# A transformer block on one core: attention output normalised with channels on partitions, its numerators and inverse sums moved by DMA, in place of transposes

## What is computed

```python
h = x @ W1 + b1                                   # q, k, v
w = softmax(q @ k.T / sqrt(8), causal)
a = (w @ v) with the heads side by side           # (512, 128)
x = layernorm(x + a @ Wp + bp)
r = sigmoid(xr @ W_r.T);  k = xk @ W_k.T          # xr, xk: x mixed with the token before it
x = layernorm(x + r * (relu(k)**2 @ W_v.T))
```

## Time and profile before

| what | us |
|---|---|
| device time, median of 3 runs (lowest, highest) | 766.25 (763.33, 769.27) |
| the profiled execution: device time | 766.06 |
| the profiled execution: span, first to last instruction | 764.3 |
| PE busy, share of the span | 621.4, 81% |
| DVE busy | 557.7, 73% |
| ACT busy | 471.6, 62% |
| POOL busy | 378.4, 50% |
| mean granted TensorE clock | 0.959 of full |

### The profile page before, as it was taken

One profiled execution on the slowest core, in us unless ns is written; L12 is line 12 of the kernel. 1 busy time (PEld: TensorE's weight loads), 2 busy tenths in 40 slices (PEclk: granted clock), 3 DMA queues, 4 the chain that ended last, 5 costly groups with the idle time before them and its releaser, 6 DMA issues.

```text
span 764.3 us, 18024 instructions
## 1 busy us (share of the span) xinstructions
PE 621.4 (81%) x6733; PEld 279.5 (37%) x6733; DVE 557.7 (73%) x1644; ACT 471.6 (62%) x918; POOL 378.4 (50%) x520
## 2 busy tenths in 40 slices
PE   2256987998988989898989898988989898977743
PEld 2013233434343435343434434343435343433232
DVE  3067777778888887879797978788887978782231
ACT  1111676586767676677777686767676766677510
POOL 6110334355655655565556464655655565455533
PEclk9999999999999999999999999999999999999755
DMA  1241213132331323241413141332323231100100
GB/s 47 96 97 49 94 54 104 44 92 66 79 93 58 112 58 115 45 124 34 118 38 118 40 127 45 75 96 58 112 59 113 54 104 29 47 17 16 29 14 14
DMA packets 65500, 53.19 MB, mean 70 GB/s; under 512 B 10882, under 2 KB 61316, under 8 KB 65412
## 3 DMA queue, kind: packets, MB, share of 16 engines
q1 hardware_dynamic: 65412, 52.03, 24.5%
HBM read 34.70 MB, written 17.30 MB: 68 GB/s over the span
## 4 chain that ended last, share of the span: by engine, by line
PE 60%; DVE 21%; ACT 8%; issue 5%; POOL 2%; DMA 2%; SPq 1%; POOLq 0%; DVEq 0%; ACTq 0%
PE ops L510 15%; DVE rowmax L661 12%; PE sps L487 10%; PE tps L451 10%; PE spare L390 8%; ACT probs L592 6%; PE spare L404 5%; PE sps L472 3%; DVE h L714 3%; PE spare L430 2%; PE spare L417 2%; PE spare L420 1%; PE spare L402 1%; DVE y L703 1%; PE spare L427 1%
## 5 line engine op out<-in xcount | busy, mean ns | idle before, releaser
L661 DVE TENSOR_REDUCE rowmax<-sps 128x1 f32<-128x512 f32 (+7 forms) x1024 | 401.3, 448 | 103.0 <-PE sps L487 102.2
L592 ACT ACTIVATE probs<-tps 128x512 f32<-128x512 f32 x640 | 346.4, 595 | 149.9 <-PE tps L451 149.9
L761 POOL TENSOR_SCALAR_AFFINE_SELECT probs<-probs 128x512 f32<-128x512 f32 x256 | 158.0, 635 | 272.6 <-ACT probs L592 272.6
L510 PE MATMUL ops<-probs,vop 128*32 128x384 f32 (+3 forms) x2048 | 175.7, 450 | 5.5 <-POOL probs L761 4.2
L451 PE MATMUL tps<-qop,kop 50*128 50x384 bf16 (+3 forms) x1024 | 127.5, 307 | 39.9 <-ACT probs L592 36.1
L487 PE MATMUL sps<-kop,qop 48*64 48x512 bf16 (+7 forms) x2048 | 130.6, 310 | 11.9 <-DMA kop<-d_parts 11.9
L472 PE MATMUL sps<-qmask,dup 64*128 64x128 bf16 (+1 forms) x640 | 69.7, 215 | 38.2 <-DVE rowmax L661 34.0
L451 PEld LDWEIGHTS tps<-qop,kop 50*128 50x128 bf16 x1024 | 34.3, 94 | 164.2 <-ACT probs L592 111.5
L510 PEld LDWEIGHTS ops<-probs,vop 128*32 128x32 f32 x2048 | 50.5, 109 | 79.9 <-issue 61.2
L487 PEld LDWEIGHTS sps<-kop,qop 48*64 48x64 bf16 x2048 | 43.1, 106 | 54.5 <-issue 19.6
L472 PEld LDWEIGHTS sps<-qmask,dup 64*128 64x128 bf16 x640 | 31.4, 95 | 80.6 <-DVE rowmax L661 74.2
(11 more groups left out here) (70 smaller groups left out, 601.7 us busy)
## 6 DMA issues: line engine op xcount, KB each, us to landing
d_parts<-qk_parts SPq DMA_DIRECT2D x16, 768.0 KB, 3.8
qop<-d_parts SPq DMA_DIRECT2D x192, 32.0 KB
qop<-d_parts SPq DMA_DIRECT2D x64, 96.0 KB
kop<-d_parts SPq DMA_DIRECT2D x192, 32.0 KB
kop<-d_parts SPq DMA_DIRECT2D x64, 96.0 KB
xa<-L_attn_x SPq DMA_DIRECT2D x16, 256.0 KB, 3.0
xres<-L_attn_x SPq DMA_DIRECT2D x16, 256.0 KB, 3.4
out<-result SPq DMA_DIRECT2D x16, 256.0 KB, 2.5
```

Of the source, the lines that this page charges most:

```text
L510: last = nc.tensor.matmul(ops[32 * t:32 * t + 32, BLK * a:SEQ], vop[:, par, a, QUARTET * half + t, hh, :], probs[:, g % 2, i, off:off + w] ...
L592: nc.scalar.activation(probs[:, g % 2, i, :], tps[:, bank(4 * GROUPS * n + 4 * g + i), :], ACT.Exp, scale=SCALE)\
L661: last = nc.vector.reduce_max(rowmax[:, par, QUARTET * half + i, a:a + 1], sps[:, bank(n), off:off + w], axis=AX_X)
L761: last = nc.gpsimd.affine_select(out=v, in_=v, compare_op=ALU.is_ge, fill=0.0, base=0, pattern=[[0, QUARTET], [1, BLK]], channel_multiplie ...
```

## The change

The numerators and sums stay with channels on partitions, as they leave PSUM, and DMA does the regrouping:

- In vop the columns of ones stand right behind each head's eight columns of v, so that ops holds for each head eight rows of numerators and eight rows of its sum. This is only an order of columns.
- The uses sums0, sums1 and attnT of spare are gone, with their transposes, DVE's reciprocals and products (L692, L695) and ACT's copy (L566).
- `move_o` (SP): osum of a half is stored to DRAM (256 KB), and after it has landed the 64 rows of numerators are read to numer (128 KB) and one row of sums per head to sums, spread over 128 partitions (16 KB, pieces of 128 bytes). Half 1 stands between the operand loads of half 1 and load_max of half 1; half 0 between the operand loads of half 0 and load_max of half 0.
- `invert_sums` (DVE, group 3): one reciprocal, 128x64, for both halves.
- `spread_inverses` (SP, behind the issue of xres and ahead of d_parts): the inverses go to DRAM (32 KB), and after that has landed they are read back with each head's row repeated on eight partitions (256 KB).
- `divide_attn` (POOL, group 4, behind the mask of group 4): one product numer by inv_rows, 128x512, straight into attnT. PE waits for it before project.

Of the diff, the declarations of the new semaphores are left out.

```diff
@@ -47,6 +47,7 @@
 PARTS = 3
+SHARE = PAIRS * SEQ // P
 LOADED = 16 * 2 * 2 * 4
@@ -63,13 +64,12 @@
     (1, 0): ("T", "max1"), (1, 1): ("A", "k"),
-    (2, 0): ("E", "key"), (2, 1): ("D", "sums1"),
-    (3, 0): ("E", "gate"), (3, 1): ("D", "attnT"),
+    (2, 0): ("E", "key"),
+    (3, 0): ("E", "gate"),
     (4, 1): ("E", "value"),
     (8, 0): ("D", "hT"),
-    (8, 1): ("T", "sums0"),
 }
@@ -183,8 +183,10 @@
         osum = sb("osum", [P, 2, SEQ])
-        inv = sb("inv", [P, 2, TT, QUARTET, 2])
-        attn = sb("attn", [P, TT, HEADS, DH])
+        sums = sb("sums", [P, 2, SHARE])
+        inv = sb("inv", [P, 2, SHARE])
+        inv_rows = sb("inv_rows", [E, SEQ])
+        numer = sb("numer", [E, SEQ])
         attnT = sb("attnT", [E, SEQ])
@@ -214,6 +216,9 @@
         d_max = nc.dram_tensor("d_max", (2, MROWS, 2, MAXIMA, QBLK), BF16, kind="Internal").ap()
+
+        d_o = nc.dram_tensor("d_o", (2, PAIRS, 2, DH, SEQ), F32, kind="Internal").ap()
+        d_inv = nc.dram_tensor("d_inv", (2, PAIRS, SEQ), F32, kind="Internal").ap()
 
@@ -318,6 +329,31 @@
 
+            def move_o(n, half):
+
+                wait(sp, o_copied, 2 * n + half + 1)
+                wait(sp, numer_in[half], 16 * n)
+                wait(sp, sums_in[half], 16 * n)
+                sp.dma_start(d_o[half].rearrange("h s d n -> (h s d) n"), osum[:, half, :])\
+                    .then_inc(o_out[half], 16)
+                wait(sp, o_out[half], 16 * (n + 1))
+                wait(sp, attn_done, n)
+                sp.dma_start(numer[E // 2 * half:E // 2 * half + E // 2, :],
+                             d_o[half, :, 0]).then_inc(numer_in[half], 16)
+                wait(sp, inv_done, n)
+                sp.dma_start(sums[:, half, :], d_o[half, :, 1, 0].rearrange("h (c n) -> h c n", n=SHARE))\
+                    .then_inc(sums_in[half], 16)
+
+            def spread_inverses(n):
+
+                wait(sp, inv_done, n + 1)
+                wait(sp, inv_in, 16 * n)
+                sp.dma_start(d_inv.rearrange("f h (c n) -> (h c) f n", n=SHARE), inv[:]).then_inc(inv_out, 16)
+                wait(sp, inv_out, 16 * (n + 1))
+                wait(sp, attn_done, n)
+                sp.dma_start(inv_rows[:], d_inv.rearrange("f h n -> (f h) n").unsqueeze(1)
+                             .to_broadcast([HEADS, DH, SEQ])).then_inc(inv_in, 16)
+
             def step(b, par):
@@ -326,6 +362,8 @@
                     load_operands(other, 1)
+                if active("D", b):
+                    move_o(before("D", b), 1)
                 if active("T", b):
@@ -334,6 +372,7 @@
                     sp.dma_start(xres[:], x[b + OFFSET["D"]].rearrange("(t p) e -> p t e", p=P)).then_inc(xres_in, 16)
+                    spread_inverses(before("D", b))
                 if active("A", b):
@@ -350,6 +389,8 @@
                     load_operands(par, 0)
+                if active("T", b):
+                    move_o(before("T", b), 0)
                 if active("S", b):
@@ -410,16 +451,8 @@
                     last = rowmax_transpose(par, 1)
-                elif use in ("sums0", "sums1"):
-                    half = int(use[-1])
-                    wait(pe, o_copied, 2 * before(stage, b) + half + 1)
-                    for t in range(TT):
-                        last = nc.tensor.transpose(spare[:, P * t:P * t + P], osum[:, half, P * t:P * t + P], ident)
-                elif use == "attnT":
-                    for t in range(TT):
-                        last = nc.tensor.transpose(spare[:, P * t:P * t + P],
-                                                   attn[:, t].rearrange("q h d -> q (h d)"), ident)
                 elif use == "project":
+                    wait(pe, attn_done, before("D", b) + 1)
                     last = tokens_by_weights(attnT, wp[:])
@@ -546,7 +579,7 @@
                 stage, use = SPARE_USES.get((g, place), (None, None))
-                if stage is None or not active(stage, b) or use in ("sums0", "sums1", "project", "value"):
+                if stage is None or not active(stage, b) or use in ("project", "value"):
                     return
@@ -560,10 +593,8 @@
                     for hh in range(2):
-                        ins = nc.scalar.copy(vop[:, 1 - par, :, :, hh, DH * hh:DH * hh + DH],
+                        ins = nc.scalar.copy(vop[:, 1 - par, :, :, hh, 2 * DH * hh:2 * DH * hh + DH],
                                              spare[:].rearrange("k (t p h d) -> k h t p d", t=TT, p=PAIRS, h=2)[:, hh])
-                elif use == "attnT":
-                    ins = nc.scalar.copy(attnT[:], spare[:])
                 elif use in ("q", "k"):
@@ -593,8 +624,8 @@
 
-            def copy_o(n, half, taken):
-                wait(act, spare_written, taken)
+            def copy_o(n, half):
+                wait(act, o_out[half], 16 * n)
                 wait(act, pv_done, GROUPS * n + CHUNKS * (half + 1))
@@ -617,9 +648,9 @@
                     if g == 1 and active("D", b):
-                        copy_o(before("D", b), 1, last_use(b, "sums1"))
+                        copy_o(before("D", b), 1)
                     if g == CHUNKS + 1 and active("T", b):
-                        copy_o(before("T", b), 0, last_use(b, "sums0"))
+                        copy_o(before("T", b), 0)
                     if active("T", b):
@@ -684,18 +715,6 @@
                                                    ALU.add, ALU.subtract).then_inc(spare_read, 1)
-                elif use in ("sums0", "sums1"):
-
-                    half = int(use[-1])
-                    wait(dve, spare_written, written)
-                    tiles = spare[:].rearrange("q (t r s h d) -> q s t r h d", t=TT, r=QUARTET, s=2, h=2)
-                    nc.vector.reciprocal(inv[:, half], tiles[:, 1, :, :, :, 0]).then_inc(inv_done, 1)
-                    wait(dve, inv_done, 2 * n + half + 1)
-                    for t in range(TT):
-                        last = nc.vector.tensor_tensor(
-                            attn[:, t, DH * half:DH * half + DH].rearrange("q (r h) d -> q r h d", h=2),
-                            tiles[:, 0, t], inv[:, half, t].unsqueeze(3).to_broadcast([P, QUARTET, 2, DH]), ALU.mult)
-                    last.then_inc(spare_read, 1)
                 elif use == "project":
@@ -708,6 +727,12 @@
 
+            def invert_sums(n):
+                for half in range(2):
+                    wait(dve, sums_in[half], 16 * (n + 1))
+                wait(dve, inv_out, 16 * n)
+                nc.vector.reciprocal(inv[:], sums[:]).then_inc(inv_done, 1)
+
             def normalise(i, n, src, dst, done_rstd, done):
@@ -721,6 +746,8 @@
                     spare_use(b, par, g, 0)
+                    if g == 3 and active("D", b):
+                        invert_sums(before("D", b))
                     if g == 7 and active("D", b):
@@ -748,7 +775,7 @@
                 last = nc.gpsimd.memset(vop[:].rearrange("k b t p h c -> k (b t p) h c")[
-                    :, :, hh, (2 + hh) * DH:(3 + hh) * DH], 1.0)
+                    :, :, hh, (2 * hh + 1) * DH:(2 * hh + 2) * DH], 1.0)
             last.then_inc(vop_cleared, 1)
@@ -786,6 +813,13 @@
                     .then_inc(step_done, 1)
+
+            def divide_attn(n, projected):
+                for half in range(2):
+                    wait(pool, numer_in[half], 16 * (n + 1))
+                wait(pool, inv_in, 16 * (n + 1))
+                wait(pool, spare_written, projected)
+                nc.gpsimd.tensor_tensor(attnT[:], numer[:], inv_rows[:], ALU.mult).then_inc(attn_done, 1)
 
@@ -827,6 +861,8 @@
                         mask_group(b, g)
+                    if g == 4 and active("D", b):
+                        divide_attn(before("D", b), last_use(b, "project"))
 
```

More of the change, by code:

```diff
@@ L244, in block_program @@
         o_copied = sem("o_copied")
+        o_out = [sem("o_out0"), sem("o_out1")]
+        numer_in = [sem("numer_in0"), sem("numer_in1")]
+        sums_in = [sem("sums_in0"), sem("sums_in1")]
         inv_done = sem("inv_done")
+        inv_out = sem("inv_out")
+        inv_in = sem("inv_in")
+        attn_done = sem("attn_done")
         xbias_done = sem("xbias_done")
```

## The result

The changed kernel takes 822.91 us (median of 4 runs, 821.87 to 824.23) where the kernel before takes 767.76 us beside it: ratio 1.0759, 95% interval 1.0712 to 1.0806. That is 7.6% slower; the forecast was 768 us with 756 to 790 as its range. The profiled execution took 823.44 us, 57.4 us more than that of before.

A forecast was written before the change was run, and what follows sets the result against it. PE, busy 81% of the span, was taken to bound the kernel. From 766.06 us, 14 full steps at +0.35 added 4.9 and steps 0, 15 and 16 took off 3.1: 767.9, said as 768, range 756 to 790.

The forecast's parts named there:

- Step 1: SP's store of osum, 256 KB, issued 325.1 after ACT's copy: lands in 3.4 us, at 328.5.
- Step 2: SP's queue after osum lands: numer and sums issues 0.4 us each; maxima's store and xres come 1.25 us later.
- Step 3: POOL's xbias starts 3.7 us after xres's issue; mask of group 3 ends 338.55, pv starts 0.25 us later than before.
- Step 4 and 5: POOL's mask of group 4 ends at 339.8; inverses ready 333.35, stored in 2.4, read back in 3.4 us: 339.2.
- Rival B: POOL's wait for inv_rows, group 4: the inverses' two transfers decide; a step +1.8 us, 788 us; chance 0.28.
- Step 6: POOL's product costs 1.27 us; project 1.1 us later, PE stands still for 0.85, v 0.95 us later.
- Step 7: SP behind spread_inverses: d_parts and half 0's operand loads some 3 us later, hidden, as are half 0's moves.
- Step 8: Group 8 on PE: sums0 goes, 0.6 us gained, counted in full.
- the gain as a whole: Transposes removed from PE: ready 1.2 us earlier from group 4 on, 0.6 us more after group 8.
- step 15: Kernel's step 15, without S: only the removed sums0 counts, at a slower clock, -1.0 us.
- the last step: Kernel's step 16, from the copy's end at 721.42: 733.1 for 734.63, so -1.5 us.

The follow-up runs named there:

- loads first: Changed kernel with SP issuing xa and xres at the head of a step, ahead of operand loads and move_o: 804.33 us, ratio 1.0511 to the kernel before.
- both limits away: Changed kernel with xa and xres issued first and no round trip of the inverses (division left out): 742.94 us, ratio 0.9703 to the kernel before.
- the added transposes: Changed kernel with 20 transposes of the identity on PE ahead of pv of group 3: 806.78 us, ratio 1.0528 to the kernel before.
- the three together: Changed kernel with xa and xres first, osum stored from ACT's queue, v before project, y's moments in group 6: 784.46 us, ratio 1.0211.
- the swap: Changed kernel with xa and xres first, v and project trading places, y's moments in group 6: 777.65 us, ratio 1.0187 to the kernel before.
- the moments: Changed kernel with xa and xres first, v before project, y's moments at the end of group 5: 755.27 us, ratio 0.9851 to the kernel before.

## Why the prediction was wrong, point by point

Where PE is bound and where the danger lies was right: the slack of 1.6 us between the mask of group 3 and pv, the mask behind xbias, xbias behind xres. What failed are two terms of the sum: the delay of xres in SP's queue was too small, and the clock was priced at nothing in the full steps. Means over the 13 steps 2 to 14, in us from the end of osum's copy:

| event | forecast | changed kernel | kernel before |
|---|---|---|---|
| numer issued | 3.4 | 3.7 | |
| maxima stored | 4.3 | 5.0 | 3.0 |
| maxima's read-back issued | 5.7 | 7.3 | 4.6 |
| xres issued | 7.3 | 8.9 | 6.1 |
| xbias starts | 11.0 | 12.4 | 9.7 |
| product starts | 14.7 | 16.5 | |
| project starts | 16.0 | 18.0 | 14.9 |

- Step 1, the store of osum: right within 0.3 us.
- **Step 2 was mis-sized, by 1.3 us**, which with the 0.3 of step 1 makes xres 1.6 us later than forecast. "0.4 taken" for each issue was 0.60 and 0.57. And I moved the store of the maxima without asking what it now stands behind: from its issue to the read-back it took 1.5 us before and 2.3 us now, right behind numer and sums. I had raised other transfers for what is ahead of them, and not this one.
- Step 3 follows from it: a wait before pv of 3.1 us in a step (47.2 us in 15), for 1.45. The mean of xbias before is 9.7, so a start of 12.4 takes all the slack and more.
- Step 4 and 5: the masks of groups 3 and 4 ran without a break and ended at 16.1, for 14.7 forecast. The inverses were ready at 8.35 as forecast, but SP, still busy with xres, sent them off only at 9.8; the store took 3.1 us and the read 3.3, and inv_rows landed at 16.3, for 14.1. So both limits end nearly together, and POOL waited for inv_rows 8.9 us in all, in 10 steps. Rival B's sign was there in part, and its time of 788 was nearer than mine, but it is not what made the loss: without the round trips 814.56 us are left. It is the limit that takes over once xres is out of the way, as loads first shows.
- Step 6: project 3.2 us later than before, for 1.1. Of the 2.0 us between forecast and trace (16.0 and 18.0), 1.7 are the later product (16.5 for 14.7).
- Step 7 held: no wait of PE for operands or for the maxima of half 0.
- Step 8 and the gain as a whole held: with both limits away the time fell by 24.5 us, for some 27 worked out.
- **The clock had no term in the full steps.** All their prices were taken from rows at full clock, the ones that follow a standstill too; only step 15 was priced at a slower one. I had put PE's standstill at 2.3 us in a step and priced it at 2.3 us.

The account, against the version with both limits away (739.64 us in its profiled execution, same PE instructions): 83.8 us more. PE's waits for POOL before pv and project are 57.9 us, for 7.6 there, which makes 50.3. The other 33.5 us are what is left of the 42.9 us by which the same matmuls took longer, after PE's other waits had become some 9 us shorter. So two fifths of these 83.8 us is the clock. That the part on the path is 33.5 is worked out; that it is at least 16 is shown by the added transposes. As an estimate, the forecast missed by 55 us: some 34 are the clock, and some 20 are PE's waits for POOL, 3.6 us a step (57.9 in 16) for the 2.3 forecast.

In the last step, too, I was too hopeful: project 12.8 us after the copy's end for 13.2 before, where I had counted 1.5 us of gain.

The expectations failed once more in the same way. For "loads first" I put two issues ahead of the operand loads and left out that SP needs 0.9 us for them, by which osum's store is issued later; for the three together I moved 1.25 us of DVE work to the one stretch without air.

What was not tried: the swap and the moments without the earlier loads, so their share is known only on top of each other; the swap and the moments in the kernel before, so how much of the 2.3% belongs to the change itself is open; and a direct measure of how the clock's fall depends on the length of a standstill.

## What to carry to other kernels

A DMA put into a queue delays everything that is issued behind it, and what matters is who waits for that: here a harmless load of the residual, behind two round trips, stopped the mask, and the mask stopped the matrix engine. Give each moved transfer a new price by what is then ahead of it, count the time that the queue's engine needs for each issue, and issue loads whose data are long known behind everything that somebody waits for. A standstill of a few microseconds of PE must be priced with the clock behind it; and before giving up a change that comes out slower, see whether its cost is only its order: the same work, with two loads, one pair of uses and eight small instructions in other places, turned 7.6% slower into 2.3% faster.

## What the runs showed of the hardware that I had not expected

- The granted clock fell to 1.2 GHz within a standstill of 4.0 us and stayed there for 10.6 us more after its end, with PE mostly busy; in the version with loads first it fell behind one of 2.57 us. It also fell at the third of three waits of 1.19, 0.53 and 1.30 us within 5 us. In the kernel before 13 steps have a wait of 1.15 us; in three of them the clock fell behind it, to come back within 4 us, and these steps took 41.0 to 42.1 us for 40.5. The Trainium skill (TensorE: Matmul & The Clock Gate, § Part 1: The HAM clock gate) says that the half rate is the engine's resting state and that activity releases it. The traces agree, from 1.00 to 0.50 in the standstill shown and back to 1.00 behind the work that followed, and the prediction had not weighed this rule against the waits it forecast.
- A store of 16 KB landed in 1.4 us (median) in the kernel before and in 2.2 us behind other transfers.
- With the operand loads still under way, osum's store of 256 KB landed 3.56 us after its issue by SP and 3.83 us after its issue by ACT (means of 13 steps); with nothing ahead, in 2.0 us. Another queue did not shorten the transfer, only the wait for its issue.
- Issuing a DMA took SP 0.60 us for 64 rows and 0.57 us for the 128 pieces of 128 bytes, for 0.30 us of an operand load.
